# A four-layer conditioned residual kernel: how the picked weights are cleared, which loads go first, and how many loads of x go out in advance

## The chip, the cores and the metric

The kernel runs on one core of a Trainium2 chip. The metric is the device time of one execution in microseconds. The core has five instruction streams that run side by side and are ordered by semaphores alone: TensorE (PE), VectorE (DVE), ScalarE (ACT), GpSimd (POOL) and SyncE (SP). SyncE only issues transfers; ScalarE issues transfers between its own instructions. The transfers of both go to the same sixteen DMA engines.

## What is computed

`x` is 128 sequences of 64 channels by 1024 time steps in f32. Four layers are added to it in turn:

```python
x = x + einsum('bct,bcd->bdt', x, W0[ids0])                 # 16 condition weights, 64x64 each, picked by ids0
x = x + mask(conv(x, K1) + D1 * x, len1)                    # long convolution, kernel from log_dt, C, log_A_real, A_imag
x = x + x @ W2.T + bias + scale * lora_b(lora_a(x))[ids2]   # linear over time (1024x1024) with 8 adapters of rank 16
x = x + mask(conv(x * m, K3) + D3 * x * m, len3)            # second long convolution
```

`ids0`, `len1`, `ids2` and `len3` are 128 integers each. K1 and K3 are made in the kernel from the parameters called `ssm` below, and the FFT of the reference is a product with Toeplitz tiles there.

## The kernel before, in words

**Stage 0** (layer 0, to about 240 us). Two sequences form a pair. For each of the 64 pairs, `pick` (64 tiles of 128x128 f32, 32 KB of each partition) holds a block diagonal of two picked 64x64 weight matrices with one added on the diagonal and a scale, so that one product gives layer 0 with its residual. The off-diagonal blocks must be zero: GpSimd clears the whole of `pick` with one memset (L604). The diagonal blocks are made by TensorE from `w0n` (the 16 weight matrices, which come in four pieces, L455) and a one-hot matrix of `ids0` (256 small matmuls in eight groups, L720), and ScalarE copies each group from PSUM into `pick` (L1167). ScalarE begins these copies behind a wait for `pick_cleared` (L1158); between the fifth and the sixth group it waits for VectorE's `angles_ready` (L1577) and takes sines and a tanh (L1162, L1163) of it. Behind each group it issues one 512 KB load of the layer-2 weight (L1118, L1170), and behind the last the adapters (L1121, L1122).

Then x goes through in 64 loads of 512 KB (two pairs, half of the time steps), issued by SyncE (`load_x`, L457 to L461) into a ring of `NXIN` = 4 slots, `xin`. `stage0(i)` runs for i = 0 to 3 with 16 loads l = 0 to 15 each; the first eight loads of each make one block of work, the last eight another. Load l may go out when TensorE has finished the matmuls of load l - 4 (semaphore `s0_summed`). For each load TensorE runs L786, ScalarE copies half of the result (L1224) and VectorE the other half (L1724) into `xq`, and after each block four stores of 960 KB take it to DRAM (L1232). Between these, in a fixed written order, TensorE turns the parameters (`turn_params`, L725 to L732, which waits for VectorE's L1635), the adapters (`turn_lot`, L764, of which LOT_A needs `lora_a`) and the layer-2 weight; GpSimd mixes rows of that weight (L675 to L684); VectorE and ScalarE make tables for the convolution kernels.

**Start of each stream.** VectorE waits for three of GpSimd's constants (L1517), then for `ids0` (L1519), makes the one-hot matrix (L1520, L1521), waits for `w0n` (L1522), adds one to its diagonals (L1525, which releases L720), waits for the other indices (L1526), makes the masks (L1527 to L1535), waits for ten ssm loads (L1567) and runs a long chain of small operations on them, each waiting for the one before (L1543 to L1635). SyncE issues ids0, len1, ids2, len3, the four pieces of w0 and then the loads of x. ScalarE issues the ten ssm loads (L1142 to L1146), the bias and, behind a wait for GpSimd's zero row (`zeros_ready`, L1153), a store of zeros (L1154). GpSimd makes its constants (L593 to L602), then clears `pick`, then waits for the layer-2 weight.

**The rest** (about 244 us to the end) runs over 16 groups of four channels, with x1 read back from DRAM: convolution (L882, L848), layer 2 (L911, L935), convolution (L1023, L1036).

The parts that the diff touches are short; the lines of the clearing and of the ring before are

```python
nc.gpsimd.memset(area(0, 32), 0.0).then_inc(pick_cleared, 1)                       # L604
at_least(sp, s0_summed, 2 * STEPS * i + 2 * (l - NXIN + 1))                        # L459
pe.wait_ge(x_loaded[l % NXIN], 16 * (STEPS // NXIN * i + l // NXIN + 1))           # L780
```

Of the kernel before, what the change touches and what calls it, by code (L numbers as in the profile page):

```python
# [34 lines left out]
P = 128  # L35
# [43 lines left out]
def build(nc, x, ids0, len1, ids2, len3, w0, ssm1, ssm3, w2, bias2, lora_a, lora_b, lora_s, out):  # L79
    with ExitStack() as ctx:  # L80
# [75 lines left out]
        tab = [t.rearrange("p (q n) -> p q n", q=HG) for t in (part_of(gbuf, 16, HG * TAB / 256), area(48, HG * TAB / 256))]  # L156
        xq = area(56, 64).rearrange("p (f k d b) -> p f k d b", f=2, k=NPART, d=C)
# [92 lines left out]
        pick_cleared = sem("pick_cleared")  # L250
        pick_summed = sem("pick_summed")
        pick_copied = sem("pick_copied")
        x_loaded = [sem(f"x_loaded{s}") for s in range(NXIN)]
        s0_summed = sem("s0_summed")
# [118 lines left out]

        def unit_of(i, half):

            return i // 2, i % 2 * 2 + half
# [72 lines left out]
        def _(sp):  # L449
            for n, row in enumerate((ids0, len1, ids2)):  # L450
                sp.dma_start(ids[:, n, :], row.rearrange("(o b) -> o b", o=1).to_broadcast([P, B])).then_inc(ids_loaded if n else ids0_loaded, 16)
            sp.dma_start(len3i, len3.rearrange("(b o) -> b o", o=1)).then_inc(ids_loaded, 16)
            for quarter in range(4):
                cols = slice(quarter * (C * C // 4), (quarter + 1) * (C * C // 4))
                sp.dma_start(w0n[0:NID, cols], w0.rearrange("i c d -> i (c d)")[:, cols]).then_inc(w0_loaded, 16)  # L455

            def load_x(i, l):  # L457

                at_least(sp, s0_summed, 2 * STEPS * i + 2 * (l - NXIN + 1))  # L459
                at0, t0 = i % 2 * 2 * STEPS + l * GPAIRS, i // 2 * HALF  # L460
                sp.dma_start(xin[:, l % NXIN], x_pairs[:, at0:at0 + GPAIRS, t0:t0 + HALF]).then_inc(x_loaded[l % NXIN], 16)  # L461
# [130 lines left out]
        def _(pool):  # L592
            nc.gpsimd.iota(pcoli, [[0, 1]], base=0, channel_multiplier=1).then_inc(iota_done, 1)  # L593
            nc.gpsimd.iota(tcoli, [[P, NBLK]], base=0, channel_multiplier=1).then_inc(iota_done, 1)
# [8 lines left out]

            nc.gpsimd.memset(area(0, 32), 0.0).then_inc(pick_cleared, 1)  # L604

# [107 lines left out]
        def _(pe):  # L713
# [58 lines left out]
            def stage0(i, first):  # L772
                for m in range(2 * STEPS):
# [5 lines left out]
                    if not odd:  # L779
                        pe.wait_ge(x_loaded[l % NXIN], 16 * (STEPS // NXIN * i + l // NXIN + 1))  # L780

                    at_least(pe, (s0_even_out, s0_odd_out)[odd], STEPS * i + m // 2 - 1)
                    for j in range(GPAIRS):
                        for kk in range(2):
                            at0, t0 = (kk * GPAIRS + j) * P, (2 * odd + kk) * P
                            mm = nc.tensor.matmul(ps[:, s, at0:at0 + P], xin[:, l % NXIN, j, t0:t0 + P],  # L786
# [329 lines left out]
        def _(act):  # L1116
# [21 lines left out]

            for v in range(2):
# [18 lines left out]
            act.wait_ge(pick_cleared, 1)  # L1158
# [879 lines left out]
```

## Time and profile before

| | us |
|---|---|
| median of 3 runs | 1580.62 |
| lowest and highest | 1577.86, 1584.58 |
| profiled execution, whole | 1581.37 |
| its span in the trace | 1579.6 |
| TensorE matmul busy | 1496.6 (95%) |
| VectorE busy | 1238.7 (78%) |
| ScalarE busy | 744.0 (47%) |
| GpSimd busy | 636.6 (40%) |
| DMA | 283.43 MB, mean 179 GB/s |

The mean granted clock of TensorE is 0.984 of full. Busy shares are means over stages with different limits: the slices of the page show where TensorE is not full, and those are the first seven of forty, each 39.5 us long. What limits one stage has to be read from the windows and waits of that stage.

### The profile page before, as it was taken

How to read it: one execution, taken by the hardware profiler on the slowest of the kernel's cores; microseconds unless marked ns; L12 is line 12 of the kernel's file. 1: busy time of each engine (PE TensorE's matmuls, PEld its weight loads, DVE VectorE, ACT ScalarE, POOL GpSimd, SP SyncE). 2: the span in 40 equal slices, each digit the busy share in tenths (PEclk: the TensorE clock that was granted, in tenths of full speed). 3: DMA queues.
4: the chain of work that ended last, by engine and by line, in shares of the span. 5: the costliest groups of instructions: out<-in, count | busy, mean ns of one | idle time of the engine just before them, and what ended most of it. 6: DMA issues, size and time to landing. Idle time of an engine off the chain costs nothing.

```text
span 1579.6 us, 36811 instructions
## 1 busy us (share of the span) xinstructions
PE 1496.6 (95%) x14983; PEld 1296.4 (82%) x14983; DVE 1238.7 (78%) x1478; ACT 744.0 (47%) x1084; POOL 636.6 (40%) x452
## 2 busy tenths in 40 slices
PE   6787777899999999999999999999999999999998
PEld 6687775778888888888888888888888888888887
DVE  7887757879696969696969787878878796969653
ACT  4544443345454545454535454545444444545433
POOL 2111122775444453535353535354545454545030
PEclk9999988999999999999999999999999999999999
DMA  7799985748493848567675747474849484848432
GB/s 226 274 356 381 360 332 174 173 94 224 93 222 98 210 118 193 135 173 155 153 175 132 196 116 201 109 206 110 215 89 231 88 227 82 234 94 224 101 134 68
DMA packets 437911, 283.43 MB, mean 179 GB/s; under 512 B 330568, under 2 KB 377168, under 8 KB 437776
## 3 DMA queue, kind: packets, MB, share of 16 engines
q1 hardware_dynamic: 388560, 172.47, 46.2%
q10 hardware_dynamic: 49216, 108.88, 19.9%
q8 instruction: 119, 1.95, 0.5%
q14 instruction: 16, 0.13, 0.0%
HBM read 159.20 MB, written 73.86 MB: 148 GB/s over the span
## 4 chain that ended last, share of the span: by engine, by line
PE 74%; DVE 9%; DMA 6%; issue 4%; ACT 3%; POOL 3%; ACTq 1%; DVEq 0%; POOLq 0%
PE ps L935 35%; PE ps L838 8%; PE ps L1023 6%; PE ps L944 5%; PE ps L911 5%; PE ps L882 4%; PE ps L1036 3%; DMA arena<-in_x_dram 3%; PE ps L848 3%; DVE arena L1839 3%; PE ps L786 3%; DMA w_scratch<-gbuf 1%; DVE gbuf L1834 1%; ACT arena L1380 1%; ACT arena L1287 1%
## 5 line engine op out<-in xcount | busy, mean ns | idle before, releaser
L935 PE MATMUL ps<-arena,w2t 128*128 128x256 f16 x4608 | 523.3, 273 | 5.9 <-DMA w2t<-w_scratch 4.7
L935 PEld LDWEIGHTS ps<-arena,w2t 128*128 128x128 f16 x4608 | 451.5, 98 | 62.8 <-DMA w2t<-w_scratch 5.0
L641 POOL TENSOR_TENSOR arena<-arena 128x68 f32<-128x68 f32 x31 | 26.6, 859 | 685.2 <-DVE arena L1889 394.1
L1932 DVE TENSOR_TENSOR arena<-arena 128x512 f16<-128x512 f32 x128 | 111.1, 869 | 115.8 <-ACT arena L1369 115.8
L786 PE MATMUL ps<-arena 128*128 128x128 f32 x1024 | 141.6, 300 | 44.0 <-DMA arena<-in_x_dram 23.5
L786 PEld LDWEIGHTS ps<-arena 128*128 128x128 f32 x1024 | 133.3, 212 | 50.1 <-DMA arena<-in_x_dram 27.1
L1356 ACT ACTIVATE arena<-ps,biasx 128x256 f32<-128x256 f32 x256 | 103.5, 472 | 137.0 <-PE ps L935 99.6
L1827 DVE SCALAR_TENSOR_TENSOR arena<-gbuf,arena 128x1024 f16<-128x1024 f32 x64 | 162.9, 2565 | 1.6 <-ACT arena L1283 1.6
L1369 ACT ACTIVATE arena<-arena 128x512 f16<-128x512 f32 x128 | 80.6, 630 | 163.3 <-DVE arena L1928 157.9
L882 PE MATMUL ps<-arena 128*128 128x512 f16 (+1 forms) x768 | 137.8, 330 | 7.8 <-DVE arena L1827 7.8
L1023 PE MATMUL ps<-arena 128*128 128x256 f16 (+1 forms) x1536 | 137.1, 246 | 1.9 <-DVE gbuf L1834 0.8
L1023 PEld LDWEIGHTS ps<-arena 128*128 128x128 f16 x1536 | 122.1, 98 | 15.6 <-DVE gbuf L1834 5.8
L882 PEld LDWEIGHTS ps<-arena 128*128 128x128 f16 x768 | 74.6, 99 | 58.8 <-issue 10.5
L1287 ACT ACTIVATE arena<-gbuf 128x1024 f16<-128x1024 f32 x64 | 67.5, 1055 | 84.5 <-DVE gbuf L1834 82.9
L1839 DVE SCALAR_TENSOR_TENSOR arena<-gbuf,arena 128x1024 f16<-128x1024 f32 x64 | 96.0, 1518 | 0.0
L1816 DVE SCALAR_TENSOR_TENSOR arena<-ps,arena 128x512 f16<-128x512 f32 x48 | 33.2, 692 | 79.0 <-ACT arena L1326 79.0
L935 PE MATMUL ps<-arena,gbuf 128*128 128x256 f16 x768 | 89.1, 273 | 0.3 <-DMA gbuf<-w_scratch 0.3
L911 PE MATMUL ps<-arena,at 128*128 128x512 f16 x384 | 85.5, 379 | 0.0
L1834 DVE COPY_PREDICATED gbuf<-mask,ps 128x1024 f32<-128x1024 uint8 x64 | 82.7, 1294 | 1.5 <-issue 1.5
L935 PEld LDWEIGHTS ps<-arena,gbuf 128*128 128x128 f16 x768 | 75.0, 98 | 9.5 <-DMA gbuf<-w_scratch 0.8
L653 POOL TENSOR_TENSOR arena<-arena 128x1024 f32<-128x1024 f32 x31 | 82.4, 2658 | 0.0
L1380 ACT ACTIVATE arena<-arena 128x1024 f32<-128x1024 f16 x60 | 63.1, 1052 | 40.4 <-DVE arena L1889 40.4
(255 smaller groups left out, 2777.9 us busy)
## 6 DMA issues: line engine op xcount, KB each, us to landing
w2t<-w_scratch ACTq DMA_DIRECT2D x96, 512.0 KB, 4.1
arena<-in_x_dram SPq DMA_DIRECT2D x64, 512.0 KB, 8.4
out_dram<-arena SPq DMA_DIRECT2D x64, 512.0 KB, 3.2
gbuf<-x_scratch SPq DMA_DIRECT2D x60, 512.0 KB, 5.6
x_scratch<-arena ACTq DMA_DIRECT2D x28, 960.0 KB, 11.0
gbuf<-w_scratch ACTq DMA_DIRECT2D x32, 512.0 KB, 4.2
arena<-krow_scratch SPq DMA_DIRECT2D x31, 512.0 KB, 8.5
arena<-tab_scratch SPq DMA_DIRECT2D x62, 68.0 KB, 2.2
```

Of the source, the lines that this page charges most:

```text
L786: mm = nc.tensor.matmul(ps[:, s, at0:at0 + P], xin[:, l % NXIN, j, t0:t0 + P], pick[:, i % 2 * 2 * STEPS + l * GPAIRS + j, :], start=True, ...
L838: mm = nc.tensor.matmul(o, ut[v][:, part, 2 * h + blk, :], xx[:, h, 2 * k + blk, :], start=(h == 0 and q == 0 and blk == 0), stop=(k == 0 ...
L882: nc.tensor.matmul(o, g1[:, h, part, d * P:(d + 1) * P], m, start=(d == 0 and q == 0), stop=False)
L911: mm = nc.tensor.matmul(ps[:, 7, :], at[:, part, k, :], xx[:, :, k, :], start=(k == 0 and q == 0), stop=(k == NBLK - 1 and q == 2))
L935: mm = nc.tensor.matmul(ps[:, bank, n * HW:(n + 1) * HW], weight(p, n, part, k), xx[:, :, k], start=(fresh and n == 0 and k == 0 and q == ...
L1023: nc.tensor.matmul(ps[:, bank, c0:c0 + w], xx[:, h, j, :], g3[:, h, part, g0:g0 + w], start=(j % 4 == 0 and xx is x3h and part == 0), stop ...
L1287: nc.scalar.activation(batch_parts(x2h[:, h]), x1_flat[:, :, h], ACT.Copy, scale=XS / FS).then_inc(x2_hi, 1)
L1356: e = nc.scalar.activation(x3part[slot + p][:, n * HW:(n + 1) * HW], ps[:, bank, n * HW:(n + 1) * HW], ACT.Identity, bias=biasx[:, o:o + 1 ...
L1827: stt(batch_parts(lo[:, h]), x1_flat[:, :, h], XS / FS, batch_parts(hi[:, h]), ALU.mult, ALU.subtract).then_inc(x1_lo, 1)
L1834: nc.vector.copy_predicated(x1_flat[:, :, h], batch_parts(mask1[:, :, :]), ps[:, b0:b0 + 2, :].rearrange("p n (m b) -> p (n m) b", b=BF)). ...
L1839: stt(batch_parts(x2l[:, h]), x1_flat[:, :, h], XS / FS, batch_parts(x2h[:, h]), ALU.mult, ALU.subtract).then_inc(x2_lo, 1)
L1932: tt(x3_quarter(x3l, h0, row), x3part[slot].rearrange("p (k h b) -> p k h b", k=2, h=2), x3_quarter(x3h, h0, row), ALU.subtract).then_inc( ...
```

## The change

- The one memset of `pick` on GpSimd is replaced by four memsets of 8 tiles each (128x1024) on GpSimd for pairs 32 to 63, behind its first iota and ahead of its others, and four of the same size on VectorE for pairs 0 to 31, ahead of everything else of VectorE. ScalarE's wait for `pick_cleared` is gone; its wait for the zero row, which GpSimd now writes after its memsets, and TensorE's picks, which follow VectorE's L1525, stand ahead of its copies as before.
- w0 comes in two pieces instead of four and is the first of SyncE's loads; ids0 is now loaded by ScalarE, ahead of its ssm loads; SyncE's len1, ids2 and len3 follow w0.
- SyncE waits for the ten ssm loads before the first load of x.
- Loads 4 to 7 of the first `stage0` go to four further slots, `x_ahead`, which lie in a part of `xq` that is written only after them. They and loads 8 to 11 no longer wait as in the ring of four: loads 0 to 7 wait for nothing, loads 8 to 11 for the load eight before, later loads for the load four before.
- VectorE waits for one of GpSimd's constants instead of three before the one-hot matrix, and for three ahead of the masks.

```diff
--- before.py
+++ after.py
@@ -154,6 +154,7 @@
         pick = area(0, 32).rearrange("p (n d) -> p n d", n=PAIRS)
         xin = area(32, 16).rearrange("p (s n t) -> p s n t", s=NXIN, n=GPAIRS)
         tab = [t.rearrange("p (q n) -> p q n", q=HG) for t in (part_of(gbuf, 16, HG * TAB / 256), area(48, HG * TAB / 256))]
+        x_ahead = area(104, 16).rearrange("p (s n t) -> p s n t", s=NXIN, n=GPAIRS)
         xq = area(56, 64).rearrange("p (f k d b) -> p f k d b", f=2, k=NPART, d=C)

         w0n = area(56, 16)
@@ -248,9 +249,11 @@
         zeros_ready = sem("zeros_ready")
         w0_ready = sem("w0_ready")
         pick_cleared = sem("pick_cleared")
+        pick_half_cleared = sem("pick_half_cleared")
         pick_summed = sem("pick_summed")
         pick_copied = sem("pick_copied")
         x_loaded = [sem(f"x_loaded{s}") for s in range(NXIN)]
+        x_ahead_loaded = [sem(f"x_ahead_loaded{s}") for s in range(NXIN)]
         s0_summed = sem("s0_summed")
         s0_even_out = sem("s0_even_out")
         s0_odd_out = sem("s0_odd_out")
@@ -371,6 +374,27 @@

             return tile.rearrange("p k (f b) -> p (k f) b", f=NF)

+        def is_ahead(i, l):
+
+            return i == 0 and NXIN <= l < 2 * NXIN
+
+        def x_slot(i, l):
+
+            return (x_ahead if is_ahead(i, l) else xin)[:, l % NXIN]
+
+        def x_slot_free(i, l):
+
+            if i == 0 and l < 2 * NXIN:
+                return 0
+            back = 2 * NXIN if i == 0 and l < 3 * NXIN else NXIN
+            return 2 * STEPS * i + 2 * (l - back + 1)
+
+        def x_arrived(i, l):
+
+            if is_ahead(i, l):
+                return x_ahead_loaded[l % NXIN], 16
+            return x_loaded[l % NXIN], 16 * (STEPS // NXIN * i + l // NXIN + (1 if i == 0 and l < NXIN else 0))
+
         def unit_of(i, half):

             return i // 2, i % 2 * 2 + half
@@ -447,18 +471,19 @@

         @block.sync
         def _(sp):
-            for n, row in enumerate((ids0, len1, ids2)):
-                sp.dma_start(ids[:, n, :], row.rearrange("(o b) -> o b", o=1).to_broadcast([P, B])).then_inc(ids_loaded if n else ids0_loaded, 16)
+            for half in range(2):
+                cols = slice(half * (C * C // 2), (half + 1) * (C * C // 2))
+                sp.dma_start(w0n[0:NID, cols], w0.rearrange("i c d -> i (c d)")[:, cols]).then_inc(w0_loaded, 16)
+            for n, row in ((1, len1), (2, ids2)):
+                sp.dma_start(ids[:, n, :], row.rearrange("(o b) -> o b", o=1).to_broadcast([P, B])).then_inc(ids_loaded, 16)
             sp.dma_start(len3i, len3.rearrange("(b o) -> b o", o=1)).then_inc(ids_loaded, 16)
-            for quarter in range(4):
-                cols = slice(quarter * (C * C // 4), (quarter + 1) * (C * C // 4))
-                sp.dma_start(w0n[0:NID, cols], w0.rearrange("i c d -> i (c d)")[:, cols]).then_inc(w0_loaded, 16)
+            sp.wait_ge(ssm_loaded, 160)

             def load_x(i, l):

-                at_least(sp, s0_summed, 2 * STEPS * i + 2 * (l - NXIN + 1))
+                at_least(sp, s0_summed, x_slot_free(i, l))
                 at0, t0 = i % 2 * 2 * STEPS + l * GPAIRS, i // 2 * HALF
-                sp.dma_start(xin[:, l % NXIN], x_pairs[:, at0:at0 + GPAIRS, t0:t0 + HALF]).then_inc(x_loaded[l % NXIN], 16)
+                sp.dma_start(x_slot(i, l), x_pairs[:, at0:at0 + GPAIRS, t0:t0 + HALF]).then_inc(x_arrived(i, l)[0], 16)

             def store_x1(i, half, part):

@@ -591,6 +616,8 @@
         @block.gpsimd
         def _(pool):
             nc.gpsimd.iota(pcoli, [[0, 1]], base=0, channel_multiplier=1).then_inc(iota_done, 1)
+            for n in range(4):
+                nc.gpsimd.memset(pick[:, PAIRS // 2 + 8 * n:PAIRS // 2 + 8 * (n + 1), :], 0.0).then_inc(pick_cleared, 1)
             nc.gpsimd.iota(tcoli, [[P, NBLK]], base=0, channel_multiplier=1).then_inc(iota_done, 1)
             nc.gpsimd.iota(trowi[:, 0:T], [[1, T]], base=0, channel_multiplier=0).then_inc(iota_done, 1)
             nc.gpsimd.memset(ident[:, :], 0.0).then_inc(iota_done, 1)
@@ -600,9 +627,6 @@
             pool.wait_ge(iota_done, 5)
             nc.gpsimd.tensor_tensor(twin[:, :], ident[:, 0:C], ident[:, C:2 * C], ALU.add).then_inc(twin_ready, 1)
             nc.gpsimd.memset(zrow[:, :], 0.0).then_inc(zeros_ready, 1)
-
-            nc.gpsimd.memset(area(0, 32), 0.0).then_inc(pick_cleared, 1)
-

             ptt = nc.gpsimd.tensor_tensor

@@ -777,13 +801,13 @@
                     blk = 2 * i + k
                     l = m // 2
                     if not odd:
-                        pe.wait_ge(x_loaded[l % NXIN], 16 * (STEPS // NXIN * i + l // NXIN + 1))
+                        pe.wait_ge(*x_arrived(i, l))

                     at_least(pe, (s0_even_out, s0_odd_out)[odd], STEPS * i + m // 2 - 1)
                     for j in range(GPAIRS):
                         for kk in range(2):
                             at0, t0 = (kk * GPAIRS + j) * P, (2 * odd + kk) * P
-                            mm = nc.tensor.matmul(ps[:, s, at0:at0 + P], xin[:, l % NXIN, j, t0:t0 + P],
+                            mm = nc.tensor.matmul(ps[:, s, at0:at0 + P], x_slot(i, l)[:, j, t0:t0 + P],
                                                   pick[:, i % 2 * 2 * STEPS + l * GPAIRS + j, :], start=True, stop=True)
                     mm.then_inc(s0_summed, 1)
                     if not odd:
@@ -1136,6 +1160,7 @@
                 act.dma_start(tab_dram[bass.ds(c * HG, HG)].rearrange("q p n -> p q n"), tab[r]).then_inc(tab_stored[r], 16)


+            act.dma_start(ids[:, 0, :], ids0.rearrange("(o b) -> o b", o=1).to_broadcast([P, B])).then_inc(ids0_loaded, 16)
             for v in range(2):
                 rows = slice(v * C, (v + 1) * C)
                 log_dt, cc, log_ar, a_imag, dd = ssm[v]
@@ -1155,7 +1180,6 @@
                           zrow[:, :].bitcast(F16).rearrange("p (s n) -> p s n", s=2)).then_inc(krow_stored, 16)


-            act.wait_ge(pick_cleared, 1)
             for dgroup in range(8):
                 if dgroup == 5:
                     act.wait_ge(angles_ready, 1)
@@ -1514,16 +1538,19 @@
             ts, tt, stt = nc.vector.tensor_scalar, nc.vector.tensor_tensor, nc.vector.scalar_tensor_tensor


-            dve.wait_ge(iota_done, 3)
+            for n in range(4):
+                nc.vector.memset(pick[:, 8 * n:8 * (n + 1), :], 0.0).then_inc(pick_half_cleared, 1)
+            dve.wait_ge(iota_done, 1)
             nc.vector.tensor_copy(pcol, pcoli)
             dve.wait_ge(ids0_loaded, 16)
             link(nc.vector.tensor_copy(idf[:, 0, :], ids[:, 0, :]))
             ts(onehot[:, :], idf[0:NID, 0, :], pcol[0:NID, :], None, ALU.is_equal)
-            dve.wait_ge(w0_loaded, 64)
+            dve.wait_ge(w0_loaded, 32)
             diag = w0n[0:NID, 0:C * C]
             diag = bass.AP(diag.tensor, diag.offset, [diag.ap[0], [C + 1, C]])
             ts(diag, diag, 1.0, None, ALU.add).then_inc(w0_ready, 1)
             dve.wait_ge(ids_loaded, 48)
+            dve.wait_ge(iota_done, 3)
             nc.vector.tensor_copy(idf[:, 1:3, :], ids[:, 1:3, :])
             nc.vector.tensor_copy(tcol, tcoli)
             nc.vector.tensor_copy(trow[:, :], trowi[:, :])
```

## Rows read from the trace of the kernel before

**Rows 1.** The page: the forty slices (part 2) and one group of instructions (part 5).

```profile
PE   6787777899999999999999999999999999999998
...
L1839 DVE SCALAR_TENSOR_TENSOR arena<-gbuf,arena 128x1024 f16<-128x1024 f32 x64 | 96.0, 1518 | 0.0
```

**Rows 2.** Windows: length, busy per engine, granted clock, DMA share, GB/s.

```profile
0.00:10.00 10.00, 0.00 (x0) 0.00 (x0) 5.76 (x2) 0.00 (x0) 9.11 (x12) 1.00 0.57 117
10.00:30.00 20.00, 19.13 (x256) 18.94 (x256) 17.16 (x83) 12.97 (x20) 0.00 (x0) 1.00 0.81 253
30.00:40.00 10.00, 8.71 (x59) 8.50 (x60) 8.56 (x39) 3.48 (x7) 0.94 (x2) 1.00 0.84 284
40.00:60.00 20.00, 14.94 (x127) 14.24 (x127) 17.08 (x33) 10.50 (x19) 2.54 (x2) 1.00 0.51 164
60.00:220.00 160.00, 125.73 (x1129) 119.95 (x1128) 124.93 (x257) 74.80 (x133) 22.15 (x20) 0.91 1.00 370
```

**Rows 3.** Timeline of the start: start us, us, engine, line, tiles, idle before.

```profile
2.76 2.42 SPq L455 DMA_DIRECT2D arena<-in_L_cond_weights_dram  x4
...
3.07 6.92 POOL L604 MEMSET arena<- 128x8192 f32 x1
...
4.39 5.68 DVE L1520 CAST arena<-arena 128x128 f32<-128x128 int32 x1 [2.22 <-DMA arena<-in_itok_B_dram]
...
5.22 152.16 SPq L461 DMA_DIRECT2D arena<-in_x_dram  x44
...
6.42 0.60 ACTq L1146 DMA_DIRECT2D gbuf<-in_L_cond_D_dram  x1
...
7.67 0.66 ACTq L1154 DMA_DIRECT2D krow_scratch<-zrow  x1
...
10.31 0.21 DVE L1525 TENSOR_SCALAR arena<-arena 16x64 f32<-16x64 f32 x1
...
10.57 19.13 PE L720 MATMUL ps<-onehot,arena 16*64 16x64 f32 x256 [10.57 <-DVE arena L1525]
...
13.24 0.74 DVE L1535 TENSOR_SCALAR past<-arena,small 128x1024 uint8<-128x1024 f32 x1
...
13.91 0.18 DVE L1543 TENSOR_SCALAR gbuf<-gbuf 128x65 f32<-128x65 f32 x1
...
23.61 0.23 DVE L1577 TENSOR_TENSOR gbuf<-gbuf 128x64 f32<-128x64 f32 x1
...
23.92 1.28 ACT L1162 ACT_TABLE_LOAD   x1
...
30.99 5.67 PE L786 MATMUL ps<-arena 128*128 128x128 f32 x32 [1.28 <-ACT arena L1167]
...
36.95 0.23 PE L728 MATMUL ps<-ident,arena 8*128 8x8 f32 x1 [0.30 <-DVE d_row L1635]
...
44.41 1.27 POOL L679 TENSOR_TENSOR gbuf<-w2t 128x512 f32<-128x512 f32 x1 [8.34 <-PE ps L764]
```

**Rows 4.** DMA issues of 0 to 60 us: count, KB each, median us to landing.

```profile
arena<-in_L_cond_weights_dram SPq DMA_DIRECT2D x4, 64.0 KB, 5.1
...
small<-in_itok_B_dram SPq DMA_DIRECT2D x1, 0.5 KB, 5.5
...
gbuf<-in_L_cond_D_dram ACTq DMA_DIRECT2D x2, 4.0 KB, 5.5
...
gbuf<-cond_lora_a_weights_dram ACTq DMA_DIRECT2D x1, 512.0 KB, 6.3
```

**Rows 5.** Chain that ended last, in order of time: start us, us, what.

```profile
65.94 12.73 DMA arena<-in_x_dram
```

**Rows 6.** Timelines of SyncE's queue and of TensorE from 54 us.

```profile
54.22 2.15 SPq L461 DMA_DIRECT2D arena<-in_x_dram  x2
...
56.23 5.85 PE L786 MATMUL ps<-arena 128*128 128x128 f32 x48 [0.26 <-ACT arena L1224]
```

**Rows 7.** Waits of 56 to 240 us: total us, times, longest us.

```profile
PE ps L786 <- DMA arena<-in_x_dram: 23.5, 12, 6.4
```


## The prediction

> **What bounds the kernel now.** I read the forty slices of the page first, then the table of windows, then the timeline of the start. The reader is to see three stretches. From slice 8 on, about 280 us, to the end TensorE is busy in nine tenths of each slice [rows 1]; nothing in the diff touches that part, so it can only be moved as a whole. From 60 to 220 us the first stage (x read, multiplied by the picked weights, x1 stored) has TensorE busy for 126 of 160 us, while the sixteen DMA engines show a share of 1.0 at 370 GB/s [rows 2]: it is bound by transfers. Before 60 us neither is full: the DMA share is 0.57, 0.81, 0.84 and 0.51 in the first four windows [rows 2]. The change works only there.
>
> The start is a chain with three places where something ends last. (a) TensorE's 256 pick matmuls start at 10.57 us, released by VectorE's L1525 at 10.31, which needs the condition weights. (b) VectorE's parameter arithmetic starts at 13.91 (L1543), right behind L1535, with no idle time of its own. (c) ScalarE needs VectorE's L1577 (23.61 plus 0.23 us) before the sines and starts their table load at 23.92; its copies of the picked weights behind them release L786 at 30.99 [rows 3]. At 36.95 the parameter transposes L728 stand in TensorE's order and wait for VectorE's L1635, the end of that arithmetic [rows 3]. So the first block of stage 0 hangs on when VectorE starts its parameter chain, more than on when the picks are done.
>
> **The clearing.** Before, one GpSimd memset of 128x8192 runs 6.92 us from 3.07 (0.865 us per 1024 elements), and VectorE's cast L1520 of 128x128, begun at 4.39, is shown for 5.68 us, to 10.07, though the 128x1024 L1535 takes 0.74: it ended when the memset did, at 9.99 [rows 3]. Nearly all of this delay lies beside another one. The last of the four pieces of w0 is issued about 0.6 us before the queue's next kind at 5.22 [rows 3] and takes 5.1 [rows 4], so it lands near 9.7, and L1525 could not have run before then. Taking the memset out of the way is worth 10.31 - 9.7 = 0.6 us by itself.
> After, GpSimd clears 4 x 1024 (4 x 0.865 = 3.5 us) behind its first iota, from about 1 to 4.5 us, and its other constants, done by 3.07 before, slip by the same 3.5 to 6.6. ScalarE's wait for the zero row slips with them, hidden behind its DMA issues, which last until 7.67 [rows 3]. VectorE clears 4 x 1024 first. No large VectorE memset is in the trace. From below, a 128x65 operation (L1543) takes 0.18 us, 0.7 us in all; from above the two-input 128x1024 L1839 takes 1.52 [rows 1], 6.1 us in all; by form L1535 with 0.74 is nearest and gives 3.0. I take 1.0 each, between L1535 and L1839: from a start near 0.7 VectorE is free at 4.7 us, before w0 lands. If the memsets of the two engines exclude one another, as L1520 and L604 did, it is 4.7 + 3.5 = 8.2 us. At the bounds, 1.4 and 6.8 us, or 10.3 with exclusion on top.
> The trace has the exclusion for a cast against a memset [rows 3]. The Trainium skill, "SBUF — State Buffer", section "Who interferes with whom", has it only for VectorE in a two-port mode or with two SBUF inputs, so the memsets would run side by side; "VectorE: DVE Perf Modes", section "Zero memsets can be issued as uint32 (trn2)", gives a memset one cycle per element, an estimate of 1.07 us for 1024 at its 0.96 GHz. By these pages VectorE would be free at about 5 us, and the sum stays as it is.
>
> **The order of the loads.** w0 is now two pieces, first on SyncE's queue. Issues there are 0.6 us apart (2.42 us for four), so the second goes at about 1.35 and with 5.1 to 5.3 us lands near 6.6 [rows 3, 4]. ids0 goes first on ScalarE's queue; L1520 shows that it landed by 4.39 when it was the first of SyncE's [rows 3], and I let it land by 5. So L1525 runs near 6.7 instead of 10.31, and the pick matmuls (19.1 us) end near 26.0 instead of 29.7. That gain of 3.6 us does not pass on, because of (b) and (c).
> The other indices: len3 is now SyncE's fifth issue, at about 2.9 us, and took 5.5 [rows 4], so they land near 8.4. VectorE's row of work from there to L1535 took from 10.52 to 13.98, 3.5 us [rows 3], and ends near 11.9.
> The ssm parameters: all ten issues of ScalarE are one issue, about 0.5 us, later. The last was issued at 6.42 [rows 3] and landed after 5.5 as the mean of the two of that line, one of them beside x loads [rows 4]; without x beside it I take 5.1, the landing time of w0: 6.9 + 5.1 = 12.0 us. The parameter chain starts at 12.0 instead of 13.91: **-1.9 us**. Two waits end almost together there, so neither alone gives more. Bounds: 11.5 (both 0.5 quicker), 12.9 (a landing 1 us late); with exclusive memsets at 1.0 us each VectorE is free at 8.2, inside it; at the upper memset bound, 10.3 + 3.5, nothing is left. So -2.4 to 0.
> Downstream: L1577 ends at 23.84 - 1.9 = 21.9. The fifth group of picks is ready at about 6.9 + 5 x 19.13 / 8 = 18.9, so ScalarE waits for the angles, starts the table load at 22.0 instead of 23.92, and its six remaining copies no longer wait for TensorE. Stage 0 starts about 2 us earlier and is stopped at L728 until 36.95 - 1.9 = 35.0 us. The block moves by 1.9.
>
> **x in advance.** SyncE waits for the ssm loads, so x starts at 12.0 instead of 5.22 us [rows 3]. It is wanted at 29; even a landing of 12.73 us [rows 5] is in time. Eight loads (4.2 MB) meet ScalarE's weight loads; GpSimd, their reader, sat 8.34 us before 44.41 waiting for TensorE's L764 with the weights already there [rows 3]: cost nothing up to that. What do eight buy? Loads 8 to 11 now go out while 0 to 3 are worked on, but load 12 again waits for load 8. When block 1 starts (56.23 us before) twelve loads have been issued either way; before, the last two went in the 2.15 us from 54.22 [rows 6] and were partly open. So the transfer-bound stretch starts with up to 1.6 loads less to move. At 370 GB/s [rows 2] one load of 0.524 MB is 1.4 us; that bounds it at 2.2 us, and the other bound is 0, since the half-used share of 0.51 before 60 us [rows 2] may already have moved them. I take **-0.8 us**. After load 12 the distance is four again, the bytes are the same, and SyncE, ScalarE and GpSimd have the same work in the same order.
>
> **Sum.** -1.9 - 0.8 = -2.7 us against the profiled 1581.37 (span 1579.6 and 1.8 around it), 1578.7. The median of the runs shown is 0.75 below that run: 1577.9, say 1578.0. Own range -4.6 to 0 by the bounds, 1576 to 1580.6, and the three runs alone spread from 1577.86 to 1584.58.
>
> **Rivals.** (1) *The head start survives.* If the four extra loads stayed ahead through the transfer-bound stretch, the 23.5 us in which TensorE waits there for x [rows 7] would shrink by up to four loads, 5.6 us: -8.3 to -10.2, 1572 or 1570. For it: these waits are the largest TensorE has there, one of 12.73 us ends the chain at 65.94 [rows 5]. Against: a share of 1.0, and a ring that closes to four at load 12. Chance 0.10.
> (2) *w0's 3.6 us pass on whole*: ssm and len3 land so early that the parameter chain starts at 10.3. With the 0.8: 1576.2. Against: the issue at 6.9, and 3.4 us for its landing. Chance 0.10.
> (3) *Late adapters, slower than before.* Eight x and eight weight loads stand in the queues which lora_a joins at about 28. About 1.6 MB of them are then left (8.7 MB asked; 16 us at 370 GB/s and 1.2 MB of weights before 12 us moved 7.1), with lora_a and lora_b 2.65 MB, 7.1 us: it lands near 35.4. L764 wants it near 43.3 - 1.9 = 41.4 (it ends at 44.41 [rows 3]). It decides from a landing of 13.4 us on, where 6.3 were taken before [rows 4]; from 16 us on the kernel is slower than before. At twice the longest landing of [rows 5], 25.5 us, L764 is 12 late, and the kernel net 9.4: 1590. For it: loads of x and of weights ask for more than 370 GB/s from 12 us on. Against: 6 us of room. Chance 0.04.
> (4) *The change does nothing*, since the memsets exclude each other at the upper bound or a landing comes after 13.5 us: 1580.6. Chance 0.16. The forecast has the other 0.60.
>
> **Chances.** What a measurement of this kernel can tell from no change is 0.5%, 7.9 us. The forecast, (2) and (4) lie inside it; (1) and (3) mostly outside. Faster 0.08, same 0.88, slower 0.04. Range for 8 in 10: 1573 to 1582.5, which leaves out (3), half of (1), and the tail of the runs' own spread.
>
> **What would show it.** Pick matmuls from about 7 us; the parameter chain from 11.5 to 12.9; L786 first at 28 to 29.5; no wait for x in the first block; TensorE's waits for x after 60 us still 20 to 24 us at a share of 1.0. The forecast is wrong if the first L882 comes not 1 to 5 us earlier than before, or if the time behind it differs by over 2 us.

## The result, and the profile after

The changed kernel takes 1577.74 us in the median of 20 runs (1574.39 to 1582.42), the kernel before 1581.44 (1577.86 to 1584.95, 20 runs): a ratio of 0.9978, 95% interval 0.9969 to 0.9988. By the ratio that is 3.5 us less (1.9 to 4.9), by the medians 3.7. Two later measurements of the same kernel gave 0.9968 (0.9958 to 0.9979) and 0.9975 (0.9962 to 0.9988). The forecast was 1578.0. Two single executions far from all others, one of the kernel before with 1609.39 us and one of ahead_only (below) with 3619.56, stand in no ratio.

Two of the forty-slice rows of the page after, to be held against [rows 1] (there TensorE's alone is shown): from slice 8 on TensorE's row is as before.

```profile
PE   7888767899999999999999999999999999999998
...
DMA  8699975648493848566675748574849483858432
```

The windows of the changed kernel (columns as in [rows 2]):

```profile
0.00:10.00 10.00, 3.88 (x53) 3.88 (x54) 7.55 (x23) 1.25 (x1) 5.88 (x15) 1.00 0.37 73
10.00:30.00 20.00, 18.70 (x224) 18.51 (x222) 17.45 (x83) 12.65 (x22) 0.00 (x0) 1.00 1.01 379
30.00:40.00 10.00, 8.37 (x64) 8.04 (x64) 8.08 (x33) 4.75 (x8) 0.86 (x2) 1.00 0.99 341
40.00:60.00 20.00, 16.76 (x120) 15.99 (x119) 14.79 (x26) 8.94 (x16) 2.54 (x2) 0.83 0.21 75
60.00:220.00 160.00, 128.67 (x1140) 122.81 (x1140) 127.01 (x261) 76.45 (x137) 22.25 (x20) 0.90 1.01 373
```

Between 10 and 40 us the DMA share is now 1.0 where it was 0.81 and 0.84, and between 40 and 60 it is 0.21 where it was 0.51 [rows 2]: the loads in advance have moved transfers to an earlier place, and left a hole behind them. The granted clock of that window is 0.83 where it was 1.00. From 60 us on share and rate are as before.

The timeline of the start, to be held against [rows 3] (start us, us, engine, line):

```profile
0.75 0.42 ACTq L1163 DMA_DIRECT2D arena<-in_itok_B_dram  x1
...
0.91 3.61 POOL L620 MEMSET arena<- 128x1024 f32 x4
...
2.10 0.91 DVE L1542 MEMSET arena<- 128x1024 f32 x1 [0.16 <-issue]
...
3.18 0.91 DVE L1542 MEMSET arena<- 128x1024 f32 x1 [0.16 <-issue]
...
5.09 0.53 DVE L1546 CAST arena<-arena 128x128 f32<-128x128 int32 x1
...
6.12 19.14 PE L744 MATMUL ps<-onehot,arena 16*64 16x64 f32 x256 [6.12 <-DVE arena L1551]
...
8.61 50.35 SPq L486 DMA_DIRECT2D arena<-in_x_dram  x14
...
10.43 0.18 DVE L1570 TENSOR_SCALAR gbuf<-gbuf 128x65 f32<-128x65 f32 x1
...
19.45 1.28 ACT L1186 ACT_TABLE_LOAD   x1
...
26.55 6.44 PE L810 MATMUL ps<-arena 128*128 128x128 f32 x32 [1.30 <-ACT arena L1191]
26.65 3.30 ACTq L1173 DMA_DIRECT2D small<-ond_scaling_factors_dram  x1
...
32.93 0.22 PE L752 MATMUL ps<-ident,arena 8*128 8x8 f32 x1
```

The picks start at 6.12 us instead of 10.57, the parameter chain (now L1570) at 10.43 instead of 13.91, stage 0 at 26.55 instead of 30.99, the parameter transposes (now L752) at 32.93 instead of 36.95. VectorE's four memsets and GpSimd's four (3.61 us) ran side by side. A VectorE memset is shown with 0.91 us, and the next starts 1.07 or 1.08 us after it started (0.16 idle): 1.0 was forecast. The estimate of 1.07 us from the Trainium skill, "VectorE: DVE Perf Modes", section "Zero memsets can be issued as uint32 (trn2)", agrees with the distance between starts, not with the 0.91 shown. By the Trainium skill, "SBUF — State Buffer", section "Who interferes with whom", memsets of the two engines don't exclude one another; here the trace agrees: both rows ran at once, while the cast of [rows 3] was held until GpSimd's memset ended.

**A slow stretch under a granted clock of 1.00.** VectorE's part of the parameters was ready still earlier: its last instruction ahead of the transposes started at 31.75 us (36.62 before). TensorE came to them only at 32.93, since its first matmuls of stage 0 ran at a slower pace. Weight loads of L810 in the windows 27 to 29, 50 to 52 and 54 to 56 us of the changed kernel (shortest, median and longest in ns):

```profile
L810 PEld LDWEIGHTS ps<-arena x11: 333/333/337, 26.7 to 28.9; 128*128 128x128 f32 x11
...
L810 PEld LDWEIGHTS ps<-arena x11: 332/333/333, 49.7 to 51.8; 128*128 128x128 f32 x11
...
L810 PEld LDWEIGHTS ps<-arena x20: 192/192/192, 53.8 to 56.0; 128*128 128x128 f32 x20
```

The profile gives the granted clock of these windows as 1.00, 0.50 and 1.00, but the loads of the first take what those of the second take. So a granted clock of 1.00 in the first microseconds of stage 0 can't be taken at its word; why the profile shows it there is not known. In all 14 profiles of this document stage 0 starts with loads of 333 ns, and the first of 192 comes 2.7 to 6.1 us later (column "pace" below). That moment differs between kernels that are the same up to there (29.84 to 32.62 us), and TensorE's parameter transposes move with it.

Four microseconds are won at 32.93, 1.7 at the first convolution matmul: L906 starts at 242.78 in this profile, where it (L882) started at 244.46 before. Where the rest went is in the windows of block 0 (columns as above):

```profile
38.00:42.00 4.00, 3.73 (x33) 3.73 (x34) 3.86 (x8) 2.54 (x6) 1.54 (x2) 1.00 0.66 213
42.00:46.00 4.00, 2.10 (x17) 1.86 (x16) 3.93 (x7) 1.41 (x3) 1.00 (x1) 0.96 0.11 40
46.00:50.00 4.00, 2.94 (x15) 2.72 (x14) 1.76 (x3) 0.72 (x2) 0.00 (x0) 0.50 0.00 0
50.00:54.00 4.00, 4.00 (x27) 4.00 (x27) 1.31 (x2) 3.31 (x6) 0.00 (x0) 0.69 0.00 0
54.00:58.00 4.00, 3.73 (x33) 3.53 (x33) 3.87 (x11) 0.92 (x3) 0.00 (x0) 1.00 0.10 33
```

From 45.8 us TensorE had its lower clock of 1.2 GHz for some 6.8 us (0.96, 0.50 and 0.69 of full in the three windows), behind a window in which it was busy for 2.10 of 4 us, waiting for VectorE. VectorE then waited for TensorE; the line of its waits (total, times, longest) reads

```profile
DVE arena L1751 <- PE ps L810: 4.9, 1, 4.9
```

and the same wait (L1724) was 2.4 us before. Those 2.5 us are what is missing of the 4.0 when block 1 begins: the first store of x1, which ScalarE issues early in block 1, starts at 57.43 instead of 58.96.

### The profile page after: what moved, and what is told of

Same layout as the page of the kernel before. It is cut to its first block, busy times and chain, and to the rows that moved or that the text cites. A ratio compares the mean times of both kernels' runs of the same rounds, so it can differ in the third digit from the quotient of the medians.

```text
span 1578.8 us, 36816 instructions
## 1 busy us (share of the span) xinstructions
PE 1502.3 (95%) x14983; PEld 1300.3 (82%) x14983; DVE 1234.1 (78%) x1482; ACT 744.3 (47%) x1084; POOL 632.7 (40%) x455
## 4 chain that ended last, share of the span: by engine, by line
PE 77%; DVE 8%; DMA 6%; issue 4%; POOL 2%; ACT 2%; ACTq 0%; DVEq 0%; POOLq 0%
PE ps L959 35%; PE ps L862 8%; PE ps L1047 7%; PE ps L968 5%; PE ps L935 5%; PE ps L906 4%; PE ps L810 3%; DMA arena<-in_x_dram 3%; PE ps L1060 3%; PE ps L872 3%; DVE arena L1866 3%; DMA w_scratch<-gbuf 1%; PE ps L744 1%; DVE gbuf L1861 1%; PE ps L923 1%
## 5 line engine op out<-in xcount | busy, mean ns | idle before, releaser
L810 PE MATMUL ps<-arena 128*128 128x128 f32 x1024 | 144.2, 303 | 41.4 <-DMA arena<-in_x_dram 23.7
L810 PEld LDWEIGHTS ps<-arena 128*128 128x128 f32 x1024 | 135.8, 215 | 47.9 <-DMA arena<-in_x_dram 28.0
L906 PE MATMUL ps<-arena 128*128 128x512 f16 (+1 forms) x768 | 138.3, 331 | 10.2 <-DVE arena L1854 10.2
L906 PEld LDWEIGHTS ps<-arena 128*128 128x128 f16 x768 | 74.8, 99 | 61.5 <-issue 13.4
## 6 DMA issues: line engine op xcount, KB each, us to landing
x_scratch<-arena ACTq DMA_DIRECT2D x28, 960.0 KB, 10.3
```

Source lines behind the costliest of these rows:

```text
L810: mm = nc.tensor.matmul(ps[:, s, at0:at0 + P], x_slot(i, l)[:, j, t0:t0 + P], pick[:, i % 2 * 2 * STEPS + l * GPAIRS + j, :], start=True, ...
L906: nc.tensor.matmul(o, g1[:, h, part, d * P:(d + 1) * P], m, start=(d == 0 and q == 0), stop=False)
```

## Experiments

All ratios are to the kernel before, measured beside each on the same chip, with 5 to 12 runs of each variant (20 in the first row of the changed kernel). They were measured in three further sets: after_again, ring4, clear_only and order_only; no_x_wait, ahead_only, mix_later and masks_on_pool; fill_pe, after_third, mix_later_ring4 and mix_later_masks. "Picks" is the start of the pick matmuls, "chain" that of VectorE's parameter chain, "turn" that of TensorE's parameter transposes, "pace" the first of TensorE's weight loads in stage 0 that takes 192 ns, "wait" VectorE's longest wait for TensorE between 40 and 60 us (2.4 at full clock), "store" the first store of x1, "conv" the first convolution matmul, all us of one profile.

| kernel | ratio | 95% interval | picks | chain | pace | turn | wait | store | conv |
|---|---|---|---|---|---|---|---|---|---|
| before | 1 | | 10.57 | 13.91 | 34.93 | 36.95 | 2.4 | 58.96 | 244.46 |
| changed (first) | 0.9978 | 0.9969 to 0.9988 | 6.12 | 10.43 | 32.05 | 32.93 | 4.9 | 57.43 | 242.78 |
| after_again | 0.9968 | 0.9958 to 0.9979 | 6.14 | 10.61 | 32.62 | 33.15 | 4.9 | 57.67 | 242.73 |
| after_third | 0.9975 | 0.9962 to 0.9988 | 6.16 | 10.58 | 32.21 | 32.97 | 4.9 | 57.48 | 239.93 |
| clear_only | 0.9999 | 0.9989 to 1.0010 | 9.64 | 12.98 | 33.86 | 35.63 | 2.4 | 57.63 | 243.75 |
| order_only | 0.9998 | 0.9986 to 1.0009 | 10.58 | 13.93 | 37.28 | 37.70 | 4.9 | 62.20 | 245.06 |
| ahead_only | 1.0005 | 0.9993 to 1.0016 | 10.57 | 13.93 | 33.91 | 36.46 | 4.1 | 60.10 | 244.58 |
| ring4 | 0.9977 | 0.9966 to 0.9988 | 6.12 | 10.35 | 29.61 | 32.46 | 3.9 | 55.99 | 239.88 |
| no_x_wait | 1.0000 | 0.9985 to 1.0016 | 6.12 | 13.62 | 32.94 | 35.63 | 4.0 | 59.24 | 244.55 |
| masks_on_pool | 0.9977 | 0.9966 to 0.9989 | 6.12 | 8.59 | 31.89 | 32.77 | 4.9 | 57.26 | 241.58 |
| fill_pe | 0.9960 | 0.9947 to 0.9973 | 6.12 | 10.43 | 31.56 | 32.66 | 2.4 | 54.67 | 238.67 |
| mix_later | 0.9949 | 0.9934 to 0.9964 | 6.12 | 10.52 | 29.84 | 32.17 | 2.4 | 52.12 | 237.02 |
| mix_later_ring4 | 0.9958 | 0.9945 to 0.9971 | 6.12 | 10.49 | 31.08 | 32.53 | 2.4 | 52.48 | 240.84 |
| mix_later_masks | 0.9956 | 0.9940 to 0.9971 | 6.12 | 8.61 | 32.68 | 33.22 | 2.4 | 53.16 | 237.24 |

One profile's "conv" scatters by about 3 us between runs of one kernel (the changed one: 242.78, 242.73, 239.93), so the ratios decide, and of the columns picks and chain, which repeat to 0.2 us. "Turn" doesn't: fill_pe and mix_later are the changed kernel up to there and have 32.66 and 32.17, against 32.93 to 33.15, because of "pace". From the first store to the end the 14 profiles take 1517.8 to 1524.8 us, in no order of the kernels. So what is won by then stays won, but one profile tells it only to some 3 us.

**The parts, each alone and one left out.** Edit of clear_only, on the kernel before (shortened: the semaphores are left out; ScalarE's wait for the clearing goes and VectorE's waits for the constants are split, as in the change):

```diff
+for n in range(4): nc.gpsimd.memset(pick[:, PAIRS // 2 + 8 * n:PAIRS // 2 + 8 * (n + 1), :], 0.0)   # behind the first iota
+for n in range(4): nc.vector.memset(pick[:, 8 * n:8 * (n + 1), :], 0.0)                              # first on VectorE
-nc.gpsimd.memset(area(0, 32), 0.0)
```

> The kernel before with only the clearing changed (four memsets on GpSimd, four on VectorE, waits as in the change); loads in their old order, ring of four. Theory of the start: w0 is the late one, L1525 at 9.3 to 9.9 instead of 10.3 us, so 0.3 to 1 us below the kernel before. Rival, the memset was the bound and the order of the loads hardly matters: 3 to 4 us below.

Edit of order_only: the change without its memsets (one on GpSimd at its old place, and ScalarE's wait for it) and without `x_ahead`.

> The kernel before with only the order of the loads changed (w0 first in two pieces, ids0 from ScalarE, x behind the ssm loads, VectorE's waits split); one GpSimd memset of all of pick at its old place, ring of four. Theory of the start with exclusion: the cast of ids0 begins at 4.4 to 5 us and is held until the memset ends at 10.0, so the picks start at 10.3 and the parameter chain at 13.5 to 13.9: 0 to 0.5 us below the kernel before. Rival, the order alone carries the gain (no exclusion, or a cast that gets in before the memset): picks at 5 to 7 us, 3 to 4 us below.

Edit of ring4, on the changed kernel (shortened: the two functions that count the semaphores go back to the ring of four with it):

```diff
-            return i == 0 and NXIN <= l < 2 * NXIN
+            return False
```

> The changed kernel with the ring of four for all loads of x (no x_ahead); clearing and order of loads as changed. Theory of the start: within 1 us of the changed kernel, so 2.5 to 4 us below the kernel before. Rival, the eight loads in advance carry the gain: within 1 us of the kernel before. My prediction's term for them was 0.8 us.

Edit of ahead_only: `x_ahead` with its functions, put into the kernel before, and nothing else.

> The kernel before with only the eight loads of x in advance (x_ahead); clearing, order of the loads and waits as before. Theory of the start: TensorE waits for no x in block 0 anyway and the ssm landings become a little later, so within 1 us of the kernel before, or up to 1 us slower. Rival, the head start is worth something by itself: 1 to 2 us below the kernel before, with fewer TensorE waits for x after 56 us than its 23.5 us.

Clearing alone gained nothing that the ratio shows (0.9999), order alone nothing (0.9998); the intervals leave each room for 2.2 us at most. The two together have 0.9977 (ring4), and in this one set the medians are 1580.44 (ring4), 1582.82 (clear_only) and 1582.56 (order_only) with 12 runs each. The timelines of the two say why. clear_only: VectorE is free at 5.6 us and sits waiting for w0.

```profile
5.09 0.53 DVE L1523 CAST arena<-arena 128x128 f32<-128x128 int32 x1
...
9.37 0.21 DVE L1528 TENSOR_SCALAR arena<-arena 16x64 f32<-16x64 f32 x1 [3.45 <-DMA arena<-in_L_cond_weights_dram]
...
12.98 0.18 DVE L1547 TENSOR_SCALAR gbuf<-gbuf 128x65 f32<-128x65 f32 x1
```

order_only: w0 is there, and the cast of ids0 is held until the memset ends at 10.0.

```profile
3.08 6.92 POOL L625 MEMSET arena<- 128x8192 f32 x1
...
4.70 5.38 DVE L1541 CAST arena<-arena 128x128 f32<-128x128 int32 x1 [3.54 <-DMA arena<-in_itok_B_dram]
...
10.32 0.21 DVE L1546 TENSOR_SCALAR arena<-arena 16x64 f32<-16x64 f32 x1
...
13.93 0.18 DVE L1565 TENSOR_SCALAR gbuf<-gbuf 128x65 f32<-128x65 f32 x1
```

Two late things end together at 10 us, and taking one away leaves the other. clear_only still had its chain 0.9 and its transposes 1.3 us earlier, which its ratio can't resolve. order_only has its chain where the kernel before has it (13.93); that its transposes come 0.75 us later (37.70) goes with its pace, 37.28. The loads in advance alone did nothing (1.0005). On top of the rest they are not told apart from nothing: ring4 and the changed kernel in one set have medians of 1580.44 and 1578.38 and ratios of 0.9977 and 0.9968, whose intervals overlap, but the two other measurements of the changed kernel, 0.9978 and 0.9975, are ring4's. The second pair, 0.9958 (mix_later_ring4) and 0.9949 (mix_later), comes from two sets. Two effects of the loads in advance are visible: in ring4 the layer-2 weights had landed by 29.23 (GpSimd's L696), in the changed kernel by 32.41 (L699), and ScalarE's issue row at 26.65 lasts 3.30 us (timeline above), where ring4's lasts 0.60. Neither cost time that the rows show: mix_later has the long issue too (3.36 us), and its transposes come at 32.17, waiting for VectorE.

**Is it x beside the small loads that made them slow?** Edit of no_x_wait, on the changed kernel:

```diff
-            sp.wait_ge(ssm_loaded, 160)
```

> The changed kernel without SyncE's wait for the ssm loads, so that the eight loads of x go out from about 3.2 us. In the changed kernel the last ssm load landed 1.8 us after its issue, where it took 5.9 us before, beside the x loads. Theory: x beside them is what made the ssm landings slow; here they take 5 to 6 us again, the parameter chain starts at 12.0 to 13 instead of 10.4 us, and the kernel loses 1.5 to 2.5 of its 3.5 us. Rival, the landings are short because fewer small loads stand in front, and x beside them costs nothing: chain at 10.4 to 10.8, time as the changed kernel within 1 us.

Times from issue to landing of the two small loads of one line (x count, KB, median us), first the changed kernel, then no_x_wait:

```profile
gbuf<-in_L_cond_D_dram ACTq DMA_DIRECT2D x2, 4.0 KB, 2.5
```

```profile
gbuf<-in_L_cond_D_dram ACTq DMA_DIRECT2D x2, 4.0 KB, 6.3
```

and in the timeline of no_x_wait the chain waits for the last of them:

```profile
3.19 55.25 SPq L485 DMA_DIRECT2D arena<-in_x_dram  x13
...
6.12 19.14 PE L743 MATMUL ps<-onehot,arena 16*64 16x64 f32 x256 [6.12 <-DVE arena L1550]
...
13.62 0.20 DVE L1569 TENSOR_SCALAR gbuf<-gbuf 128x65 f32<-128x65 f32 x1 [1.55 <-DMA gbuf<-in_L_cond_D_dram]
```

The first theory held and went further than it said: nothing of the 3.5 us can be seen any more (1.0000, 0.9985 to 1.0016; masks_on_pool, which ran beside it, has 0.9977). One wait that holds back 4 MB of x for 5.4 us is a part without which the gain is gone, though the picks start at 6.12 here too.

**Does VectorE's work now set the chain?** Edit of masks_on_pool, on the changed kernel: VectorE's nine mask instructions go to GpSimd, behind a semaphore, and ScalarE waits for them once before block 1.

> The changed kernel with the nine mask instructions (2.3 us of VectorE ahead of the parameter chain) on GpSimd. The ssm loads landed at 8.6 us and the chain started at 10.4. Theory that VectorE's own work, not a landing, now sets the chain's start: it starts at 8.6 us or just behind, TensorE's parameter transposes 0.5 to 1.5 us earlier (the picks' end at 25.3 us binds next), 0.5 to 1.5 us below the changed kernel. Rival, GpSimd's work beside the chain holds up its operations by the shared port: no gain or a loss.

The chain did start at 8.59, directly behind the last ssm landing, 1.8 us earlier; the transposes came at 32.77, 0.2 us earlier, and the ratio is that of the changed kernel. TensorE got to its place in the order no earlier: the picks end near 25.2 in both, and the pace comes at 31.89 (32.05 there). So VectorE's 1.8 us lay beside TensorE's own way to the transposes.

**The clock and the hole in block 0.**

> The changed kernel once more, for its profile and beside the others. Theory of the start (the gain is the earlier parameter chain, L1570 at 10.4 instead of 13.9 us, and nothing else): 3 to 4 us below the kernel before, picks again from 6.1 us. The clock: in the first profile the granted clock fell to half from 45.8 to 52.6 us, beside a DMA share of 0.00, and block 1 began only 1.5 us earlier though the parameters had been 4.0 us earlier. If that fall belongs to the kernel it stands there again; if it is a matter of the execution, the clock is full there in this one and block 1 begins 3.5 to 4 us earlier.

> The changed kernel once more, beside fill_pe and the two others: 3 to 4.5 us below the kernel before, the clock at half from 45.5 to 52.5 us.

The fall came in all three profiles of the changed kernel, at the same place, with VectorE's wait at 4.9 us each time. Edit of fill_pe, on the changed kernel, in TensorE's stage 0 (12 transposes that compute nothing, at two places where TensorE is idle):

```diff
+                    if first and m in (7, 11):
+                        pe.wait_ge(turned_copied, 1)
+                        for _ in range(12):
+                            nc.tensor.transpose(ps[:, 4, 3 * P:4 * P], ident[:, :], ident[:, :])
                     at_least(pe, (s0_even_out, s0_odd_out)[odd], STEPS * i + m // 2 - 1)
```

> The changed kernel with 12 transposes of the identity into an unused corner of a PSUM bank ahead of the two places of block 0 (load 3 and load 5, about 38.3 and 44.9 us) where TensorE waits 1.63 and 1.90 us for VectorE's L1751; GpSimd's mix as in the changed kernel. In both profiles of the changed kernel the granted clock fell to half near 46 us, behind a stretch of 42 to 46 us in which TensorE was busy 2.1 of 4 us, and VectorE then waited 4.93 us for TensorE where it waited 2.44 before. Theory that the idle time of TensorE brings the fall: the clock stays full or falls later, that wait is 2 to 3 us again, block 1 starts 1.5 to 2.5 us earlier, 1 to 2.5 us below the changed kernel. Rival, the fall has nothing to do with the idle time (a stretch that comes with every execution at that moment): it stands there again and the time is the same or, by the fill, up to 1 us longer.

Windows of fill_pe, to be held against those above:

```profile
38.00:42.00 4.00, 4.00 (x36) 4.00 (x37) 3.86 (x7) 2.28 (x5) 1.81 (x2) 1.00 0.68 234
42.00:46.00 4.00, 3.18 (x27) 2.75 (x25) 3.93 (x7) 1.42 (x3) 0.73 (x1) 1.00 0.06 20
46.00:50.00 4.00, 2.96 (x27) 2.99 (x28) 1.56 (x3) 1.84 (x3) 0.00 (x0) 1.00 0.00 0
50.00:54.00 4.00, 3.75 (x34) 3.58 (x33) 3.90 (x9) 2.86 (x6) 0.00 (x0) 1.00 0.00 0
54.00:58.00 4.00, 4.00 (x43) 3.75 (x42) 3.87 (x10) 1.19 (x2) 0.00 (x0) 1.00 0.69 225
```

TensorE did more work, none of it of use, and the kernel went to 0.9960; VectorE's wait is 2.4 us again and the first store comes at 54.67 instead of 57.43 to 57.67. After_third, in the same set, has 0.9975, and the two intervals overlap (median 1575.34 against 1578.62), so of the time the experiment gives the direction. In this profile the granted clock stays at 1.00 in block 0. That the fill did it is likely and not shown: it is one profile, and the kernel before and clear_only kept their clock in theirs without a fill. The Trainium skill, "TensorE: Matmul & The Clock Gate", section "Why this matters for your kernels", says that long gaps between bursts of matmuls bring the lower clock. The trace agrees in part: the changed kernel's fall stands right behind gaps, but of 1.90 and 1.06 us, shorter than those the page speaks of, and the kernel before has gaps of 1.91 and 1.26 us in that place and no fall.

Edit of mix_later, on the changed kernel:

```diff
-                pool.wait_ge(w2_turned, 1 if q == 0 else n - 1)
+                pool.wait_ge(w2_turned, 2 if q == 0 else n - 1)
```

> The changed kernel with one wait moved: GpSimd's first mix of weight rows waits for the second turned lot instead of the first. In the changed kernel its two 1.27 us additions stand beside VectorE's L1678 and L1679, shown with 1.40 and 1.46 us for 0.36 and 0.44. Theory that the two engines hold each other up on VectorE's path in block 0: those two fall to 0.4 us, block 1 starts up to 2 us earlier, 0.5 to 2 us below the changed kernel. Rival, what VectorE gains TensorE's clock or the full DMA queues take back: no difference.

In the changed kernel GpSimd's addition and VectorE's operation on 128x272 stand side by side:

```profile
40.38 1.27 POOL L703 TENSOR_TENSOR gbuf<-w2t 128x512 f32<-128x512 f32 x1 [7.11 <-PE ps L788]
40.41 1.40 DVE L1678 TENSOR_SCALAR gbuf<-gbuf,small 128x272 f32<-128x272 f32 x1
...
41.73 1.27 POOL L705 TENSOR_TENSOR gbuf<-gbuf,w2t 128x512 f32<-128x512 f32 x1
41.84 1.46 DVE L1679 SCALAR_TENSOR_TENSOR gbuf<-gbuf 128x272 f32<-128x272 f32 x1
```

and in mix_later the same two VectorE operations, with GpSimd's addition 5 us later:

```profile
39.65 0.35 DVE L1678 TENSOR_SCALAR gbuf<-gbuf,small 128x272 f32<-128x272 f32 x1
...
40.04 0.44 DVE L1679 SCALAR_TENSOR_TENSOR gbuf<-gbuf 128x272 f32<-128x272 f32 x1
...
45.64 1.26 POOL L703 TENSOR_TENSOR gbuf<-w2t 128x512 f32<-128x512 f32 x1 [12.39 <-PE ps L788]
```

2.1 us of VectorE's path go, the granted clock stays at 1.00 in block 0, the first store comes at 52.12, and the ratio is 0.9949 (medians 1574.76 against 1581.57). The changed kernel itself was not in this set; masks_on_pool, whose ratio is the changed kernel's, was, and its 9 runs (1576.95 to 1579.27) lie wholly above mix_later's 5 (1573.18 to 1576.11). One changed number is worth more than 2 us here. How much of it is VectorE's path and how much the kept clock, this run doesn't part.

> mix_later without the loads in advance (ring of four). ring4 alone was at 0.9977 of the kernel before, the changed kernel at 0.9968 and 0.9978: not told apart. If the eight loads in advance are worth my 0.8 us or nothing, this is within 1 us of mix_later's ratio of 0.9949. If they are worth 2 us, it is 0.996 or above.

> mix_later with the masks on GpSimd too. masks_on_pool started the chain at 8.6 us, but TensorE's parameter transposes came at 32.77, only 0.2 to 0.4 us earlier, behind the picks' end at 25.2 us. So nothing more than mix_later: 0.994 to 0.9955. Rival: without the half clock in block 0 the 1.8 us of VectorE's head start count, 0.9935 to 0.994.

Neither added anything to it; mix_later_ring4 is discussed above, mix_later_masks (0.9956) had its transposes at 33.22 and kept the full clock. Their medians, 1575.18 and 1575.51, are 3.4 and 3.1 us below that of after_third in the same set (1578.62), so the gain of the later mix came again.

## Why the prediction was right, and where two of its terms were not

*What bounds the kernel*: right for the long stretches. The change moved the start alone, TensorE's waits for x after 56 us are 23.7 us (25.4 and 22.6 in the two later profiles, 23.5 before), and from the first convolution matmul to the end it takes 1336.0 us against 1335.1. Of the three places in the start, (c) was read wrongly. At 23.84 and 23.90 two things end together, VectorE's L1577 and ScalarE's own copy of the fifth group of picks, and the table load at 23.92 stood behind the second; in the changed kernel it starts at 19.45, ahead of the same VectorE instruction (L1604, at 20.11). Two rows of the kernel before:

```profile
23.31 0.59 ACT L1167 ACTIVATE arena<-ps 64x512 f32<-64x512 f32 x1
...
27.22 0.20 DVE L1597 TENSOR_SCALAR gbuf<-gbuf 128x64 f32<-128x64 f32 x1 [0.83 <-ACT gbuf L1163]
```

So the gain of the picks did pass on, once the chain was early enough. The table load moved by 4.47 us (19.45), stage 0 by 4.44 (26.55), both as the picks (4.45), not by the 1.9 of the text; and VectorE's chain, 3.5 us earlier at its start, no longer waited the 0.83 us for ScalarE. Where the chain stays late, the picks are not enough: in no_x_wait they start at 6.12, the chain at 13.62, and stage 0 at 29.19.

*The clearing*: right. w0 was the late one behind the memset, which clear_only shows (it waits until 9.37; the text had 9.7), and with the new order alone L1525's instruction stays where it was, held by the memset (order_only, 10.32 against 10.31).

*The order of the loads*, the term of -1.9 us: mis-sized. The chain started 3.5 us earlier, not 1.9. The step that failed is "without x beside it I take 5.1" for the landing of the last ssm load: that 5.1 was itself taken from loads which stood among others, and the two loads of that line took 1.8 and 3.3 us with no 512 KB load in the queues (2.5 in the median row). The same holds for len3, 4.3 instead of 5.5 us. With these two, the mechanism of rival (2), w0's gain passed on and the parameter chain at 10.3, is what happened; I gave it 0.10, and argued against it with the very number that fell. Its time, 1576.2, is 1.5 us below the measured one.

*x in advance*, the term of -0.8 us: not shown. It is not told apart from nothing, nor from 2 us. The hole was missed: behind loads 8 to 11 nothing is left to move in the second half of block 0 (share 0.00 from 46 to 54 us). That the loads cost nothing is what the rows show, though ScalarE stood 3.5 us behind its own issues.

*Missed altogether*: the clock. The text named no way for TensorE to lose time in block 0. In the profiles of the changed kernel it loses some there twice: 0.9 us at the transposes by the slow start, and 2.5 of the 4.0 us won by the fall at 45.8.

*The sum*: -2.7 against a measured -3.5, and the nearness is in part luck. The head of the kernel gained 4.0 us at the transposes where 1.9 was forecast. If the kernel before keeps its clock as in its one profile, the fall takes 2.5 of them, block 1 begins 1.5 us earlier, and 2.0 of the measured 3.5 us have no place in this account. If it loses its clock in most executions, as order_only and ahead_only did in theirs, which take the same time, the fall is no cost of the change and the 4.0 pass on nearly whole. The kernel before has one profile, so which of the two it is stays open.

*Signs named*: the picks from about 7 us came at 6.12; L786 at 28 to 29.5 was wrong (26.55), the chain at 11.5 to 12.9 was wrong (10.43); no wait for x in block 0, waits of 20 to 24 us behind it (but for the 25.4 of after_again), and a first convolution matmul 1 to 5 us earlier were right. Rivals (1), (3) and (4) did not happen: lora_a landed 8.6 us after its issue (6.3 before), and TensorE had no wait for it.

## What to carry to other kernels

Where two late things end together, each alone can be worth too little to measure and the pair more than the sum: price them together, and test them one at a time only to learn which pair it is. When reading what released an instruction, look for a second thing that ended within a tenth of a microsecond, on the engine itself too. Before taking a landing time from a row, ask what stood in the queues beside that load; a few small loads that start a chain are worth a wait that keeps megabytes off the queues for 5 us. A gain ahead of a stage that runs in turns between two engines has to be followed through it: behind idle places in TensorE's row its clock can be at half for several microseconds, and a mix that may as well run later should not stand beside the other engine's path.

## What the runs showed of the hardware that was not expected

- A 4 KB load landed 1.8 to 3.3 us after its issue with no 512 KB load in the queues, and 6.3 us (median of two) with eight 512 KB loads beside it.
- VectorE operations of 0.35 and 0.44 us (mix_later) are shown with 1.40 and 1.46 us beside GpSimd additions of 1.27 us; memsets on both engines did not hold each other up.
- With the loads in advance in the queues, one of ScalarE's issue rows of tiny loads lasts 3.30 us, and its next operation comes 3.49 us late; without them the row lasts 0.60 us (ring4).
- TensorE's first matmuls of stage 0 ran at the pace of a granted clock of 0.50 (weight loads of 333 ns, later 192) while the profile shows 1.00, for 2.7 to 6.1 us in each of the 14 profiles.
- The granted clock fell to half in block 0 in 8 of 14 profiles (three of the changed kernel, ring4, order_only, ahead_only, no_x_wait, masks_on_pool). Two kept it with the same holes in TensorE's row (before, clear_only), and the four in which the hole ahead of it was filled or shorter (fill_pe, mix_later and its two variants) all kept it. That ties the fall to the holes; what decides whether it comes, no run shows. The 24 transposes of fill_pe compute nothing, and the kernel was not longer for them.
